# Graph attention, linear mixing and top-2 experts on one core: two first stages made one, and a weighted sum split between two engines

## The reference

```
gate_logits = xf @ Wg + bg
top_w, top_i = jax.lax.top_k(gate_logits, 2)
top_w = softmax(top_w)
for e in range(8):
    h = gelu(xf @ W1[e] + b1[e])            # 256 -> 1024
    out = out + w_dense[:, e:e+1] * (h @ W2[e] + b2[e])   # 1024 -> 256
```

## Time and profile before

| what | us |
|---|---|
| median of 3 runs (lowest, highest) | 6074.43 (6071.44, 6104.11) |
| the profiled execution | 6074.89 |
| its span in the profile | 6073.2 |
| PE busy | 4404.4 (73%) |
| POOL busy | 3514.6 (58%) |
| DVE busy | 3263.1 (54%) |
| ACT busy | 2788.6 (46%) |

### The profile page before, as it was taken

The page is one execution under the profiler, slowest core; times in us unless marked ns, Lnnn a source line. Parts: engine busy times, 40 slices in busy tenths (PEclk is TensorE's granted clock), DMA queues, the critical chain, the costliest instruction groups (busy, mean ns, idle before and its releaser), DMA issues. The chain is left out here.

```text
span 6073.2 us, 86394 instructions
## 1 busy us (share of the span) xinstructions
PE 4404.4 (73%) x20831; PEld 3240.0 (53%) x20831; DVE 3263.1 (54%) x8933; ACT 2788.6 (46%) x8556; POOL 3514.6 (58%) x3659
## 2 busy tenths in 40 slices
PE   7288888888888888646666666666655256988997
PEld 4266666666666667534444444444444144656665
DVE  3377767777777777745454555554544463222222
ACT  2276666767666777334444444433333121222222
POOL 0377777777777775047777777777777201333332
PEclk9699988999989999768787877777777658999999
DMA  4688888888888886345555555556665333111111
GB/s 161 175 244 237 238 238 242 243 240 245 240 238 243 244 242 188 105 127 141 142 141 141 142 142 141 139 148 167 167 167 158 108 98 137 44 44 43 44 45 33
DMA packets 689328, 975.28 MB, mean 161 GB/s; under 512 B 390218, under 2 KB 482216, under 8 KB 688606
## 3 DMA queue, kind: packets, MB, share of 16 engines
q0 software_dynamic: 228304, 716.77, 41.3%
q1 hardware_dynamic: 459998, 252.19, 15.0%
q10 hardware_dynamic: 560, 1.05, 0.0%
HBM read 899.62 MB, written 64.56 MB: 159 GB/s over the span
## 5 line engine op out<-in xcount | busy, mean ns | idle before, releaser
L806 POOL DMA_INDIRECT walk_ring<-s_h,walk_index x3320 | 3195.7, 963 | 1354.7 <-issue 931.4
L967 PE MATMUL walk_pM<-walk_ring,walk_hit 128*128 128x262 f32 (+1 forms) x9960 | 2774.3, 432 | 12.3 <-ACT walk_ring L831 7.6
L967 PEld LDWEIGHTS walk_pM<-walk_ring,walk_hit 128*128 128x128 f32 x9960 | 2037.1, 212 | 417.5 <-issue 71.0
L831 ACT ACTIVATE walk_ring<-walk_ring 128x128 f32<-128x128 f32 (+1 forms) x6640 | 2134.3, 414 | 5.4
L1197 DVE TENSOR_TENSOR acc<-walk_pM,acc 128x520 f32 (+1 forms) x1494 | 833.3, 558 | 591.6 <-PE walk_pM L967 570.5
L821 ACT ACTIVATE walk_ring<-walk_gap 128x40 f32<-128x40 f32 (+1 forms) x249 | 54.1, 258 | 1907.8 <-DVE walk_gap L1159 1907.8
L871 PE MATMUL walk_pC<-all_ident,walk_best 128*84 128x128 f32 (+1 forms) x166 | 62.2, 375 | 1063.4 <-DVE walk_best L1115 965.5
L871 PEld LDWEIGHTS walk_pC<-all_ident,walk_best 128*84 128x84 f32 (+1 forms) x166 | 20.7, 125 | 1125.8 <-issue 1125.8
L1164 DVE TENSOR_TENSOR walk_hit<-walk_pK,walk_meta 128x512 f32<-128x512 f32 x830 | 560.8, 676 | 12.1 <-PE walk_pM L967 0.5
L1897 ACT ACTIVATE expert_hT<-expert_pG,expert_b 128x128 f32<-128x128 f32 x840 | 228.3, 382 | 724.4 <-PE expert_pG L1967 724.3
L1115 DVE TENSOR_TENSOR walk_best<-walk_ring,walk_dt 128x40 f32<-128x40 f32 (+1 forms) x249 | 47.1, 216 | 861.3 <-DMA walk_ring<-s_h,walk_index 861.3
(11 more groups left out here) (308 smaller groups left out, 4031.9 us busy)
## 6 DMA issues: line engine op xcount, KB each, us to landing
walk_hitT<-s_places SPq DMA_DIRECT2D x166, 640.0 KB, 6.6
walk_ring<-s_h,walk_index POOLq DMA_INDIRECT x3320
expert_w<-in_fw_dram SPq DMA_DIRECT2D x16, 1024.0 KB, 13.1
walk_goal<-walk_target SPq DMA_DIRECT2D x830, 6.0 KB
walk_goal<-walk_target SPq DMA_DIRECT2D x830, 1.5 KB
walk_xk<-s_xT SPq DMA_DIRECT2D x98, 128.0 KB, 2.7
walk_resets<-s_resets SPq DMA_DIRECT2D x415, 20.0 KB
s_h<-node_h_out SPq DMA_DIRECT2D x7, 1056.0 KB, 4.3
```

What stands on the lines that cost most here:

```text
L806: pool.indirect_dma_start(ring[:, r % RS, t, :], None, table, bass.IndirectOffsetOnAxis(ap=index[:, r % TS, t:t + 1], axis=0)).then_inc(ro ...
L831: last = nc.scalar.activation(row, row, ACT.Copy, scale=ring[:, r % RS, t, at + FH:at + FH + 1])
L967: last = nc.tensor.matmul(pM[:, b, a, 0:WIDE], hit[:, (r * CGROUPS + g) % HBUF, t % GROUP, :], ring[:, r % RS, t, a * HALF_ROW:a * HALF_RO ...
```

## The change

**One first stage.** `node_pass` and `edge_pass` become `first_pass`. Norms are made part by part of ten tiles: the first part's statistics, variances, root and Newton step come before the loop, those of later parts are spread over the loop (`prepare_norm`). The edge chain is cut into steps, and each is put behind the normal work of a certain tile (`edge_work`, once for DVE, once for PE). SP stores the tables between the row stores.

```
+        T_ENDS, T_WALK, T_WINDOWS, T_PLACE, T_TURN = 1, 4, 8, 12, 22
...
+                def prepare_norm(t):
+                    if t == 0:
+                        measure(1, range(*XPARTS[1]))
+                    c = t // XP + 2
+                    if c < len(XPARTS) and t % XP >= XP // 2:
...
+                        measure(c, range(first, min(first + 2, hi)))
+                    c = t // XP + 1
+                    if c < len(XPARTS) and t % XP == 0:
+                        variances(c)
+                    if c < len(XPARTS) and t % XP == 2:
+                        inverse_roots(c)
...
+                def edge_work(t):
+                    if t == T_ENDS:
+                        find_ends()
+                    if t == T_WALK:
+                        plan_walk()
+                    if t == T_WINDOWS:
+                        keep_windows()
+                    if T_PLACE <= t < T_PLACE + 8:
+                        edge_step(t - T_PLACE)
+                    if T_TURN <= t < T_TURN + len(TABLES):
+                        copy_table(t - T_TURN)
...
+                list_firsts()
+                measure(0, range(*XPARTS[0]))
+                variances(0)
+                find_rows()
+                attention_weights()
+                inverse_roots(0)
+                for t in range(U):
+                    norm(t)
+                for t in range(NT):
+                    dve.wait_ge(multiplied, t + 1)
+                    nc.vector.tensor_copy(k["attn1"][:, t, :], pA[:, t % 2, 0:2 * HEADS1]).then_inc(a_copied, 1)
+                    if t + U < NT:
+                        norm(t + U)
+                    prepare_norm(t)
+                    edge_work(t)
...
+                def store_tables(i):
+                    if i == 2:
+                        sp.wait_ge(windows_ready, 1)
...
+                    if i == 4:
+                        sp.wait_ge(places_ready, 1)
...
+                        sp.wait_ge(resets_ready, 1)
...
+                    if i == 6:
+                        sp.wait_ge(table_copied, len(TABLES))
...
```

```
-    SX = 4
+    SX = 6
...
                 for e in range(NEXP):
+                    if e == 1:
+                        sp.wait_ge(x_turned, 2)
+                    if e >= 2:
+                        sp.wait_ge(weights_in[e - 1], 32)
+                        sp.sem_inc(experts_in, 1)
...
                     if e == 0:
                         sp.dma_start(b2[:, :, :], d["fb2"].partition_broadcast(P)).then_inc(bias_in, 16)
-                for e in range(NEXP):
-                    sp.wait_ge(weights_in[e], 32)
-                    sp.sem_inc(experts_in, 1)
+                        sp.wait_ge(weights_in[e], 32)
+                        sp.sem_inc(experts_in, 1)
+                sp.wait_ge(weights_in[NEXP - 1], 32)
+                sp.sem_inc(experts_in, 1)
...
                     if t >= SX:
                         pool.wait_ge(x_turned, t - SX + 1)
-                        pool.wait_ge(total_ready, t - SX + 1)
+                        pool.wait_ge(out_ready, t - SX + 1)
...
                 def scatter_totals(t):
+                    pool.wait_ge(out_ready, t + 1)
+                    pool.wait_ge(total_in[t % SZ], 16 * (t // SZ + 1))
+                    nc.gpsimd.tensor_tensor(total[:, t % SZ, :], out[:, t % 2, :], total[:, t % SZ, :], ALU.add).then_inc(total_ready, 1)
                     pool.wait_ge(total_ready, t + 1)
...
                     dve.wait_ge(down_done, t + 1)
-                    nc.vector.tensor_tensor(out[:, t % 2, :], pO[:, t % 2, 0:D], b2[:, e, :], ALU.add).then_inc(out_ready, 1)
-                    return e
-
-                def add_total(t, e):
-                    dve.wait_ge(out_ready, t + 1)
-                    dve.wait_ge(total_in[t % SZ], 16 * (t // SZ + 1))
-                    nc.vector.scalar_tensor_tensor(out=total[:, t % SZ, :], in0=out[:, t % 2, :], scalar=xin[:, t % SX, bass.ds(e + D, 1)],
-                                                   in1=total[:, t % SZ, :], op0=ALU.mult, op1=ALU.add).then_inc(total_ready, 1)
+                    if t >= 1:
+                        dve.wait_ge(out_ready, t)
+                    nc.vector.tensor_tensor(sums[:, :], pO[:, t % 2, 0:D], b2[:, e, :], ALU.add).then_inc(out_read, 1)
+                    dve.drain()
+                    if t >= 2:
+                        dve.wait_ge(total_ready, t - 1)
+                    nc.vector.tensor_scalar(out[:, t % 2, :], sums[:, :], xin[:, t % SX, bass.ds(e + D, 1)], None, ALU.mult).then_inc(out_ready, 1)
...
                     if t + 2 < TT:
                         copy_tokens(t + 2)
-                    if t >= 1:
-                        add_total(t - 1, expert[t - 1])
-                    expert[t] = take_out(t)
-                add_total(TT - 1, expert[TT - 1])
+                    take_out(t)
...
-                        pe.wait_ge(out_ready, t - 1)
+                        pe.wait_ge(out_read, t - 1)
```

484 lines of the change are left out of this document (245 added, 239 removed).

## The result

| what | us |
|---|---|
| before: median of 4 runs (lowest, highest) | 6084.08 (6071.44, 6104.11) |
| after: median of 4 runs (lowest, highest) | 5866.98 (5866.44, 5882.91) |
| ratio, 95% interval | 0.9647, 0.9612 to 0.9681 |
| after: the profiled execution, its span | 5882.91, 5881.2 |
| PE, POOL, DVE, ACT busy after | 4391.3, 3603.4, 3257.1, 2791.0 |

The changed kernel is faster by 217 us by the medians. Its profiled execution is the slowest of its four, 16 above the median.

What follows compares the result with a forecast made beforehand. PE was taken to bound the node stage, small steps and DMAs the edge stage, and a circle of waits the experts. Terms summed to -206.3 from the profiled 6074.9 us, giving 5869; the 8-in-10 range was 5840 to 5935.

Steps and rivals of the forecast that it cites:

- First product: Start of the first stage: norms made in parts let PE's first product come at 30.6 instead of 43.4 us, -12.8.
- Table transposes: Product loop: two more PE transposes in each of 21 tiles, all on the path, +5.8 us.
- DVE's steps in the loop: Product loop: DVE's norm and edge work exceeds the slack in tiles 0, 1, 4 and 12 to 19, +9 us.
- The edge stage: Between last row store and walk's first load: the separate edge stage goes, table stores hidden behind the loop, -66.2 us.
- Start of the experts: Expert stage start: PE waits only for the first expert's loads and b2, not 16 loads, -32.1 us.
- The period: Expert stage, 104 steps: PE sets the beat at 8.03 us per tile instead of 9.145, -116.0 us.
- the old circle: Old expert stage: PE awaits tokens, their gather a scatter's landing, the scatter DVE's add, queued behind copying these tokens; 9.145 us.
- Under the weight loads: First 60 us or so of the expert stage: weight loads lengthen the circle for four or five tiles, +6 us.
- POOL as the bound: Rival, expert stage: slower totals and add make POOL's circle 8.2 to 8.6 us, total 5908; chance 0.2.
- First stage bound by DVE: Rival, first stage: DVE bursts cost 29 us instead of 9, table stores 11 at the end, total 5900; chance 0.08.
- Tokens further ahead do not help: Rival, expert stage: gathers five tiles ahead serve no sooner than three, period stays 9.145 us, total 5985; chance 0.07.
- POOL's cost of changing between descriptors and arithmetic: Rival, expert stage: switching costs POOL microseconds twice per tile; at a 4 us add, total 6158, slower than before; chance 0.03.

Runs made afterwards that it cites:

- e8: Changed kernel with the second part's statistics made before the loop and ACT's root one tile later; 5851.40 us in one run.
- e9: Changed kernel with statistics earlier, root later, table stores spread over three rounds and b2 on its own semaphore; third chip, 6767.30 us, ratio 0.9683.
- e5: Changed kernel with SP's old order, all 16 weight loads issued before PE is told of the first expert; 5889.23 us in one run.
- e11: Changed kernel with weight and add back on DVE and tokens three tiles ahead, weights still expert by expert; third chip, one run, 6932.35 us.
- e3: Changed kernel with tokens three tiles ahead again (SX = 4), add still on POOL; 5881.60 us, ratio 0.9687.
- e4: Changed kernel with weight and add back on DVE one tile later, tokens still five tiles ahead; 5880.26 us, ratio 0.9676.
- e10: Changed kernel with tokens four tiles ahead (SX = 5); third chip, one run, 6809.45 us.
- e6: Changed kernel with two more POOL adds per tile into a spare buffer; 5946.36 us in one run.
- e1: Changed kernel with the old expert stage put back, new first stage kept; 6035.25 us, ratio 0.9927 against the kernel before.
- e2: Changed kernel with the old first two stages put back, new expert stage kept; 5918.44 us, ratio 0.9740 against the kernel before.
- e7: Changed kernel with POOL instead of SP issuing the six stores of resets and through, when ready; 5871.14 us in one run.
- e12: The changed kernel unaltered, run again on the third chip; 6774.99 us, ratio 0.9694 against the kernel before there.

## Why the prediction was right, point by point

The forecast was 5869 us, and the median is 5866.98. It was a sum of terms, and they did not all hold. That it came within 2 us of the median is luck, as told below the terms.

**First product, -12.8: right.** 30.87 us, where "near 31" was to be seen; -12.6.

**Table transposes, +5.8: right, a little large.** Products of the 21 tiles stand 2.555 instead of 2.335 us apart, 21 x 0.22 = +4.6.

**DVE's steps in the loop, +9: right in its kind, a little small, and in part in other places.** Without transposes and hole, the loop's surplus is 24.7 - 4.6 - 8.2 = 11.9 us. The row of long steps in tiles 12 to 19, for which the sum had about 4 us, cost 0.2 in all. The steps behind tiles 1, 2 and 3 cost 6.7 (5.36, 3.80 and 4.53 us), those behind 20 and 21 3.8. A long step of DVE can hurt in three ways, and the prediction had one, DVE's late copy for ACT. It left out ACT's root, which waits for DVE's variances with the copy behind it, and PE's fall to the lower clock. e8 gives 6 to 8 us of it back.

**The edge stage, -66.2: right in size, wrong in one sentence.** From the last product to the walk's first load it is 10.7 instead of 77.7 us, -67.0. But "SP's table stores are hidden behind the product loop" failed. The prediction looked at `meta` and `index`, the last ones, and at the loop's end; it priced a short cover at the end, 11 us at most. The cost came in the middle: the stores of `resets` and `through` fill the DMA engines, a row store (issued 2.3 us late behind them) waits its turn, and with it a buffer, ACT and PE. Price: 8.3 + 5.0 - 2 x 2.555 = 8.2 us, of which 2.4 are PE's lower clock behind the hole. The walk's first load was said to come near 172 and came at 181.1; e9, with the stores spread and the bursts gone, has it at 168.3.

**Start of the experts, -32.1: right**, -31.8; e5 shows its 27 us as the cost of the loads' order alone.

**The period, 8.03: right.** 834.0 / 104 = 8.02, with 7.98 in the steady state. The circle was put at 7.4 and is 7.1: the add takes 0.72 instead of 0.6, but the totals are ready about 2.8 us after their issue, where 3.2 was taken. The reason given for the old circle holds too, as e11 shows row by row; what the prediction did not say is that either edit alone would have cut it.

**Under the weight loads, +6: nothing.** The circles were longer than 8 us for four tiles, as forecast, but the buffers took up 17.9 us of it. The price exists: some 17 us with tokens three ahead (e3), 13 with the add on DVE (e4), 4 to 8 with four ahead (e10).

**The end, 0: -6.9.** From the last scatter to the end of the span it was 11.6 and is 4.7. This was in no term.

Added up, the first stage fell 9.4 us short of its terms (-54.8 instead of -64.2), and the expert stage gave 13.7 more (-155.7 instead of -142.1), of which 6.9 are the tail and most of the rest the loads. The forecast's nearness to the median is owed to these two cancelling, and to how the walks fell in the other runs: the profiled execution's span lies 12 us above the forecast. Each term was within 10 us.

**The walks were to take the same time, and in the profiles they took 18.5 us more.** No instruction there differs. In the runs on the first two chips the same stretch, from the walk's first load to the experts' first DMA, took 4803.9 (e8), 4806.9 (e3), 4807.5 (e6), 4807.7 (e5), 4812.1 (e1), 4817.7 (e2), 4819.8 (e7), 4824.7 (e4) and 4828.7 (the changed kernel), without relation to which first stage ran in front. It is scatter of about 25 us, larger than several terms of the sum; what causes it was not looked into.

**The rivals.** POOL as the bound: its mechanism is real (e6), its threshold is an add of some 1.6 us by the estimate above, and 0.72 is far from it. First stage bound by DVE: no; DVE is busy for half of the loop (69.6 of 141 us, where the prediction's "about 80" was high). Tokens further ahead do not help: false as the rival put it (e11 against e4, 8.95 against 7.98 us in mid-stage), but with the add on POOL they change only the time of the weight loads (e3). POOL's cost of changing between descriptors and arithmetic: the add takes the same 0.72 us in every tile, and 0.83 us lie between its end and the scatter's start, as 0.85 did before between DVE's add and the scatter. There is no such cost to be seen.

## What to carry to other kernels

Where a late engine waits for a tile's own gather, look not at the gather's length but at what stands behind the waiting instruction on its queue: here an add whose operands were there already. Gathering further ahead or moving the add to another engine, either alone cuts the circle, and the second cure buys only the phase in which transfers are slow, so price them apart. And when small stores are hidden behind a loop that stores too, count the DMA engines' busy share and not only the issue times and the bytes: a burst of small pieces that is early enough still holds up the loop's own stores, and here spreading it over the loop was the cure (e9), and another issuing engine was not (e7).

## What was not expected of the hardware

**The tail.** From the issue of the last scatter to the end of the span it is 4.7 us in the changed kernel:

```profile
5876.51 1.01 POOL L1939 DMA_INDIRECT out_dram<-expert_total,all_token_out  x1 [0.83 <-POOL expert_total L1937]
```

Its span ends at 5881.2. Before it is 11.6 (6061.63 to 6073.2), with the same instructions behind the scatter. It was 11.5 or 11.6 in all four kernels with `SX = 4` (before, e1, e3, e11), 4.7 in those with `SX = 6`, and 4.3 with `SX = 5`. It goes with the number of token buffers and with no other edit that was made; why, no run shows.

**The chip.** On the third chip the walks take 5718.5 us (e12) instead of 4803.9 to 4828.7, and the GB/s row of the profile's page reads about 200 instead of 240 over the first walk. The first stage (walk's first load at 181.49 against 181.08) and the expert stage (873.3 against 871.4) last the same. The change's gain in microseconds is thus nearly the same on both, 211 and 217, and its ratio is not (0.9694 and 0.9647).

**Full DMA engines at 76 GB/s.** A DMA share of 1.05 stood beside 76 GB/s in one window and 284 in another of the same stretch. In that stretch a row store took 9.4 us to land instead of 5.3. The share told it, and the bytes did not.
